# Attention value products in pairs of quads, a zero-fed opening for TensorE, and re-placed loads and steps

## Chip, core and metric

The kernel runs on one NeuronCore of one Trainium2 chip. The metric is the device time of one execution in microseconds (us), as the median of several runs. The engines are TensorE (PE, matmuls; its weight loads are shown as PEld), VectorE (DVE), ScalarE (ACT), GpSimd (POOL) and SyncE (SP), which here only issues DMAs. The text calls a busy or issue record by the line of the kernel that made it (L898 is line 898).

## The reference

32 batches of 100 queries (x, width 256) and 361 keys (ctx). Per batch:

```python
d = layernorm(x)                              # no weights
q = d @ Wq.T + bq;  k = ctx @ Wk.T + bk;  v = ctx @ Wv.T + bv     # 16 heads of 16
attn = softmax(q k^T)  (no scale);  z = attn v
x = x + (layernorm(z + d) * gamma + beta)
n = layernorm(x)
f = layernorm(n) * ln_g + ln_b
w = top 2 of 8 experts of softmax(f @ rW + rb), renormalised
x = x + n + sum_e w_e * (gelu(f @ W1_e + b1_e) @ W2_e + b2_e)
```

## The kernel before

The attention is a software pipeline over the 32 batches. Each engine runs `iteration(turn, i)` for i from -3 to 39, and each iteration has 12 **moments** s = 0 to 11. In iteration i the engines work on several batches at once: they project keys and queries of batch i+3, take row scores and row maxima of batch i+1, take transposed scores, exponentials and products with the values of batch i, and normalise batches i-1 to i-3. Where a step stands is written by hand in tables: `PE_PLACE`, `ACT_PLACE`, `DVE_PLACE`, `POOL_PLACE`, `SP_PLACE` give each step a moment (12 and more means the next iteration), `START` overrides them for batch 0 and `TAIL` for the last three. Within one moment an engine goes through its steps in the order of its `iteration` function. Places only fix the order of work on each engine; the meeting of engines is by semaphores. `SCORES_LAG, GUARD_LAG, VALUES_LAG = 3, 6, 9` place the scores, the guard and the products of a quad.

The steps that matter here, for a batch:

- **Keys** (`project_keys`, L853, PE): two fp32 products (t = 0, 1) of 361 columns each into the PSUM bank `pj[1]`. ACT writes the bf16 high part (`keys_high`, L1100) and the full value (L1104) from the bank; POOL subtracts (`k_rest`, L786), ACT makes the middle part (L1113), POOL the low part (`k_low`, L789). SP then copies the parts into `k_stack` with six DMAs of 192 KB (L653; for batch 0 in `first_stacks`, L599). Queries go the same way (L871, L1089, L1093, L793, L1109, L770) and SP copies them with six DMAs of 64 KB (L645).
- **Values** (`project_values`, L884, PE). DVE adds the bias into a tile `v_raw` (`values_biased`, L1342 and L1347) and then cleans it into `v_aug` (`values_cleaned`, L1354). `v_aug` holds each head as 16 values, a one and zeros, 32 columns in all.
- **Row scores and maxima**: 16 matmuls into two banks (`score_rows`, L898), each followed by a maximum on DVE (`row_max`, L1360). The maxima are split in three bf16 parts (`m_rows`, 48 columns) and transposed on PE (`max_transposed`, L908), copied by ACT (L1240), and stored by SP into the query stack (L635).
- **Transposed scores** (`scores`, L917): 12 groups g of four matmuls; ACT takes the exponential of each into `p_t` (`exponentials`, L1183). Three groups make a **quad** of heads. DVE guards a finished quad (`guard`, L1365).
- **Products with the values** (`values`, L929): one quad at a time, at g = 0, 3, 6, 9 with a lag of 9 moments. Twelve fp32 matmuls (24 instructions) whose weights are 32 columns wide, four of them side by side in the array. `p_t` has two slots, so the exponentials of a quad wait for the products two quads earlier.
- **z and what follows**: ACT copies z (L1254), PE transposes it (L937), DVE normalises (L1371 to L1382), SP stores it to DRAM (`zout`, L638: 1,600 pieces of 64 bytes) and loads it back (`zin`, L632), POOL adds (`u`, L798), and two layer norms follow on DVE, POOL and ACT. SP writes the result twice (`zf`, L657 and L660).

SP issues everything in one order. In an iteration this order is: zin, q, k (all moment 2), ctx (3, the load of the keys' input, L628), zout (4), zf (7), max (10). POOL's order is q_low, rstd2, k_rest, u, k_low, rstd, xb, y, q_rest, m_rest, m_low.

x comes in six loads. The first two are issued at the start. `X_LOAD_AT` gives the others to ACT (L1208); load 2 (batches 12 to 21, 1,000 KB) is issued at (i, s) = (-2, 10). The first layer norm's sums are made on DVE, one batch a time (`x_sums`, L1300), where `X_SUM_AT` says; the first of load 2 at (-1, 6). When all batches of a load are summed, eight small steps make the variance (`x_variance_step`, L1310 to L1324).

After the attention a second phase gathers tokens by expert and runs the experts over 57 tiles of 128 tokens (L976 to L999, gather L706, scatter L721). The change does not touch its work, only where some of its buffers lie.

## Time and profile before

| | |
|---|---|
| Median of 3 runs | 846.84 us (845.5 to 849.79) |
| The profiled execution, its own time | 850.93 us |
| Its span in the profile | 848.7 us |
| Mean granted clock of TensorE | 0.943 |
| PE busy | 755.9 us (89%) |
| DVE busy | 631.7 us (74%) |
| ACT busy | 563.4 us (66%) |
| POOL busy | 535.6 us (63%) |

The attention pipeline fills about the first 560 us of the span, its even stretch runs from about 188 to 515 us, and the experts' tiles take the rest. A record says how long an instruction took and, in brackets, how long its engine sat idle before it and what ended that. Matmuls overlap, so their records are longer than their distance; the chain that ended last gives the distance. Records of SPq and ACTq are the issuing of a DMA, not its transfer.

### The profile page before, as it was taken

To read this page: it belongs to the slowest core of one execution; us is meant where nothing else is said; L and a number is where in the kernel's file an instruction comes from. 1 tells how busy PE (TensorE), PEld (TensorE's weight loads), DVE (VectorE), ACT (ScalarE), POOL (GpSimd) and SP (SyncE) were. 2 spreads that over 40 slices of the span, in tenths; PEclk is the share of its full clock that TensorE was granted. 3 is DMA by queue.
4 is the path that set the end of the run, shared out by engine and by line. 5 is a ranking of instruction groups with operands and counts; after the bars stand their busy time and mean duration, and the time that the engine had idled before them with its cause. 6 is when DMAs were issued, how large, how long until landed. Compare 5 with 4: busy or idle time off the path is not lost.

```text
span 848.7 us, 26242 instructions
## 1 busy us (share of the span) xinstructions
PE 755.9 (89%) x8056; PEld 586.7 (69%) x8057; DVE 631.7 (74%) x1779; ACT 563.4 (66%) x1469; POOL 535.6 (63%) x609
## 2 busy tenths in 40 slices
PE   3689999999999999999999997565979888999994
PEld 2456667767777777777777675344968787999994
DVE  7488998889899998998998898875446673454441
ACT  3346777888888887888888885533655544666662
POOL 3323667677677676876777775317456555777773
PEclk9989999999999999999999999855989998999998
DMA  6756575768768677677687676621334333443441
GB/s 186 170 122 144 125 159 123 161 148 179 161 150 189 140 172 165 152 170 169 147 183 160 160 169 147 195 59 43 57 55 63 51 46 56 75 63 57 67 62 21
DMA packets 154000, 104.43 MB, mean 123 GB/s; under 512 B 68364, under 2 KB 149560, under 8 KB 153816
## 3 DMA queue, kind: packets, MB, share of 16 engines
q1 hardware_dynamic: 133462, 77.42, 41.8%
q0 software_dynamic: 10944, 14.10, 10.3%
q10 hardware_dynamic: 9538, 12.23, 5.1%
q8 instruction: 28, 0.46, 0.2%
q14 instruction: 28, 0.23, 0.1%
HBM read 36.65 MB, written 17.33 MB: 64 GB/s over the span
## 4 chain that ended last, share of the span: by engine, by line
PE 62%; DMA 11%; DVE 8%; issue 6%; POOL 6%; SPq 4%; ACT 2%; DVEq 1%; ACTq 0%; POOLq 0%
PE s_row L988 9%; PE pj L884 8%; PE pj L853 8%; PE s_row L898 7%; PE s_t L917 7%; PE zt L929 7%; PE pj L999 4%; PE zt L999 4%; PE pj L871 3%; SPq L653 2%; DMA stack_x<-in_x 2%; DMA out_x<-index_space,idx_s 2%; DMA zscr<-zn 2%; DVE negmax L1360 2%; DMA stack_x<-k_part 2%
## 5 line engine op out<-in xcount | busy, mean ns | idle before, releaser
L1360 DVE TENSOR_REDUCE negmax<-s_row 100x1 f32<-100x361 f32 x512 | 251.5, 524 | 24.8 <-PE s_row L898 18.9
L1183 ACT ACTIVATE p_t<-s_t 128x400 f32<-128x400 f32 x384 | 187.9, 499 | 85.8 <-PE s_t L917 77.6
L898 PE MATMUL s_row<-stack_x,q_stack 125*128 125x361 bf16 x512 | 133.2, 322 | 18.7 <-DVE negmax L1360 12.8
L721 POOL DMA_INDIRECT out_x<-index_space,idx_s x57 | 92.2, 1617 | 76.3 <-ACT index_space L1168 34.6
L917 PE MATMUL s_t<-q_stack,stack_x 128*128 128x100 bf16 x1536 | 129.4, 211 | 10.9 <-ACT p_t L1183 8.7
L917 PEld LDWEIGHTS s_t<-q_stack,stack_x 128*128 128x128 bf16 x1536 | 93.5, 99 | 57.3 <-issue 30.9
L988 PE MATMUL s_row<-w_qkv,v_aug 128*128 128x128 f32 x912 | 117.8, 285 | 1.2 <-DVE v_aug L1455 1.2
L988 PEld LDWEIGHTS s_row<-w_qkv,v_aug 128*128 128x128 f32 x912 | 113.0, 202 | 1.8 <-DVE v_aug L1455 1.7
L1365 DVE TENSOR_SCALAR p_t<-p_t 128x1200 f32<-128x1200 f32 x128 | 100.0, 781 | 12.8 <-ACT p_t L1183 12.7
L884 PE MATMUL pj<-w_qkv,ct 128*128 128x256 f32 x384 | 106.0, 399 | 0.0
L853 PE MATMUL pj<-ct,w_qkv 128*128 128x361 f32 x256 | 96.1, 500 | 10.3 <-DMA bk_s<-in_bk 9.2
L929 PE MATMUL zt<-p_t,v_aug 128*32 128x100 f32 (+1 forms) x3072 | 96.7, 261 | 1.0 <-DVE p_t L1365 1.0
L929 PEld LDWEIGHTS zt<-p_t,v_aug 128*32 128x32 f32 (+1 forms) x3072 | 67.3, 113 | 34.9 <-issue 33.3
L1162 ACT ACTIVATE w_qkv<-s_row,b_k 128x128 f32<-128x128 f32 x228 | 64.8, 367 | 27.0 <-PE s_row L988 24.5
L898 PEld LDWEIGHTS s_row<-stack_x,q_stack 125*128 125x128 bf16 x512 | 46.8, 101 | 50.5 <-DVE negmax L1360 34.8
L706 POOL DMA_INDIRECT q_part<-zf_d,idx_g x57 | 68.2, 1196 | 17.8 <-issue 15.7
L884 PEld LDWEIGHTS pj<-w_qkv,ct 128*128 128x128 f32 x384 | 66.5, 193 | 6.4 <-issue 1.1
L853 PEld LDWEIGHTS pj<-ct,w_qkv 128*128 128x128 f32 x256 | 46.0, 198 | 27.5 <-issue 11.0
L1154 ACT ACTIVATE w_qkv<-pj,lnb_c,lng_c 128x128 f32<-128x128 f32 x57 | 26.1, 457 | 51.1 <-PE pj L976 44.2
L1455 DVE TENSOR_SCALAR v_aug<-w_s 128x1024 f32 x57 | 40.2, 706 | 23.7 <-issue 22.6
L798 POOL TENSOR_TENSOR u<-z_in,td 100x256 f32<-100x256 f32 x32 | 45.7, 1427 | 18.5 <-DMA z_in<-zscr 17.8
L767 POOL TENSOR_TENSOR m_rest<-negmax,m_rows 100x16 f32<-100x16 f32 x32 | 36.4, 1139 | 32.4 <-ACT m_rows L1248 32.4
(232 smaller groups left out, 1423.8 us busy)
## 6 DMA issues: line engine op xcount, KB each, us to landing
stack_x<-k_part SPq DMA_DIRECT2D x192, 192.0 KB, 3.6
q_stack<-q_part SPq DMA_DIRECT2D x192, 64.0 KB, 2.0
ct<-in_ctx_t SPq DMA_DIRECT2D x32, 361.0 KB, 4.3
stack_x<-in_w ACTq DMA_DIRECT2D x8, 512.0 KB, 6.7
w_s<-in_w ACTq DMA_DIRECT2D x14, 256.0 KB, 2.9
zscr<-zn SPq DMA_DIRECT2D x32, 100.0 KB
z_in<-zscr SPq DMA_DIRECT2D x32, 100.0 KB
zf_d<-zf_s SPq DMA_DIRECT2D x32, 100.0 KB
```

The source lines that it names most:

```text
L706: pool.indirect_dma_start(zg[:, k.ring, :], None, zf_rows[0:n], bass.IndirectOffsetOnAxis(idx_g[:, k.ring:k.ring + 1], 0), bounds_check=n ...
L721: pool.indirect_dma_start(out_rows[0:n], bass.IndirectOffsetOnAxis(idx_s[:, k.slot:k.slot + 1], 0), ys[:, k.slot, :], None, bounds_check=n ...
L853: last = nc.tensor.matmul(pj[1][:, 0:KEYS], wk_s[:, c, t * 128:t * 128 + 128], ct[:, a.slot, c, 0:KEYS], start=(c == 0), stop=(c == 1))
L884: last = nc.tensor.matmul(bank[:, kt % 2 * D:kt % 2 * D + D], ct[:, b.slot, c, kt * 128:kt * 128 + 128], wv_s[:, c, :], start=(c == 0), st ...
L898: nc.tensor.matmul(s_row[h % 2][:, 0:KEYS], q_stack[0:MROW, b.slot, h, :], k_stack[0:MROW, b.slot, h, 0:KEYS], start=True, stop=True).then ...
L917: last = nc.tensor.matmul(s_t[g % 2][:, j * Q:j * Q + Q], k_stack[:, b.slot, h, kt * 128:kt * 128 + 128], q_stack[:, b.slot, h, 0:Q], star ...
L929: last = nc.tensor.matmul(zt[32 * j:32 * j + 32, quad * Q:quad * Q + Q], v_aug[0:n, b.slot, kt * H + 4 * quad + j, :], p_t[0:n, quad % 2, ...
L988: last = nc.tensor.matmul(p_h[k.slot][:, j * 128:j * 128 + 128], w1_k[k.slot][:, c * HF + j * 128:c * HF + j * 128 + 128], zgt[:, k.slot, ...
L999: last = nc.tensor.matmul(p_y[k.slot][:, 0:D], hidt[:, k.slot, c * 128:c * 128 + 128], w2_s[:, bass.ds(e, 1), c, :].rearrange("p e f -> p ...
L1183: nc.scalar.activation(p_t[:, quad % 2, kt, :], s_t[g % 2][:, 0:4 * Q], ACT.Exp).then_inc(exp_done, 1)
L1360: v.tensor_reduce(negmax[:, b.slot, h:h + 1], s_row[h % 2][0:Q, 0:KEYS], AXIS.X, ALU.max, negate=True).then_inc(max_done, 1)
L1365: v.tensor_scalar(p_t[:, quad % 2], p_t[:, quad % 2], 0.0, None, ALU.max).then_inc(p_ready, 1)
```

## The change

1. `values` runs two quads in one go, at g = 3 (quads 0 and 1) and g = 9 (2 and 3), and waits for the guard of the second. `p_t` gets a third slot, addressed by `ring(b, quad)`.
2. `v_raw` is gone: the bias is added straight into `v_aug`, which is then cleaned in place. Buffers of the second phase move into `k_rest` and `p_t`.
3. `m_rows` is 128 columns wide (80 of them zeros), and so is the transposition of the maxima.
4. At the start PE runs eight products of zeros (400 columns, fp32), one more after the first keys, three after the first queries. The first keys' second half goes into the bank `zt` and doesn't wait for the first half to be read; ACT reads both high parts first. PE waits only for its own weights there, not for the bias.
5. x loads 2 to 5 are issued later (load 2 at (-1, 8) in place of (-2, 10)), and their sums made five an iteration from (0, 1) on; the variance of load 2 at i = 2 in place of 1; three small loads (`later_loads`) at i = 0 in place of -1.
6. The place tables change. On SP the order becomes zin, q (moment 0), zf (1), k (5), ctx (6), zout (9), max (11). POOL's and DVE's orders stay. On ACT drow, k0, k1 and zft go ahead, the maxima's copy and q_mid go behind the next exponential. On PE dt, zft and router go ahead.

```diff
-X_LOAD_AT = {(-2, 10): 2, (0, 0): 3, (0, 6): 4, (1, 0): 5}
-X_SUM_AT = {(-1, 6 + n): 12 + n for n in range(6)}
-X_SUM_AT.update({(0, 1 + n): 18 + n for n in range(4)})
-X_SUM_AT.update({(1 + (n >= 3) + (n >= 7), (1, 3, 9, 1, 3, 9, 10, 1, 3, 9)[n]): 22 + n for n in range(10)})
+X_LOAD_AT = {(-1, 8): 2, (0, 2): 3, (0, 8): 4, (1, 2): 5}
+X_SUM_AT = {(n // 5, (1, 4, 7, 9, 10)[n % 5]): 12 + n for n in range(20)}
...
+def ring(b, quad):
+    return (b.slot + quad) % 3
...
-        p_t = sb(es, "p_t", [128, 2, KT, 4 * Q])
+        p_t = sb(es, "p_t", [128, 3, KT, 4 * Q])
-            m_rows = sb(att, "m_rows", [Q, 3 * H], BF16)
+            m_rows = sb(att, "m_rows", [Q, 128], BF16)
...
+            def keys_bank(a, t):
+                return zt if a.known and a.index == 0 and t == 1 else pj[1]
...
-                    if isinstance(turn, int) and i == -1:
+                    if isinstance(turn, int) and i == 0:
                         later_loads()
...
+                def run_idle(n):
+                    for _ in range(n):
+                        nc.tensor.matmul(tr[:, 0:G * Q], zt_s[:, 0:128], zt_s[:], start=True, stop=True)
...
-                    nc.tensor.matmul(tr[0:3 * H, 0:Q], m_rows[:], ident_bf[:], start=True, stop=True).then_inc(mt_done, 1)
+                    nc.tensor.matmul(tr[:, 0:Q], m_rows[:], ident_bf[:], start=True, stop=True).then_inc(mt_done, 1)
...
-                    pe.wait_ge(p_ready, G * b.index + quad + 1)
+                    if quad % 2 == 0:
+                        pe.wait_ge(p_ready, G * b.index + quad + 2)
...
                 pe.wait_ge(memsets, 4)
+                pe.wait_ge(zeros_ready, 1)
+                run_idle(8)
...
-                        if n.valid() and g % KT == 0:
+                        if n.valid() and g in (KT, 3 * KT):
+                            values(n, g // KT - 1)
                             values(n, g // KT)
...
-                        after(act, pv_done, G * b.index + quad - 1)
-                    nc.scalar.activation(p_t[:, quad % 2, kt, :], s_t[g % 2][:, 0:4 * Q], ACT.Exp).then_inc(exp_done, 1)
+                        after(act, pv_done, G * b.index + quad - 2)
+                    nc.scalar.activation(p_t[:, ring(b, quad), kt, :], s_t[g % 2][:, 0:4 * Q], ACT.Exp).then_inc(exp_done, 1)
...
-                    after(dve, v_ready, b.index)
+                    after(dve, pv_done, G * (b.index - 2))
...
-                    v.scalar_tensor_tensor(v_aug[:, b.slot, :, 0:DH], v_raw[:], 0.0, v_raw[:], ALU.max, ALU.min).then_inc(v_ready, 1)
+                    biased = v_aug[:, b.slot, :, 0:DH]
+                    v.scalar_tensor_tensor(biased, biased, 0.0, biased, ALU.max, ALU.min).then_inc(v_ready, 1)
...
-                        if isinstance(turn, int) and i in (1, 4) and 4 <= s < 12:
-                            x_variance_step({1: 2, 4: 3}[i], s - 4)
+                        if isinstance(turn, int) and i in (2, 4) and 4 <= s < 12:
+                            x_variance_step({2: 2, 4: 3}[i], s - 4)
...
-PE_PLACE = {"v0": 1, "v1": 2, "v2": -1, "k0": 5, "k1": 10, "dt": 3, "q": 6, "z": 7, "zft": 3, "router": 6, "max": 12}
-ACT_PLACE = {"drow": 2, "k0": 6, "k1": 11, "dt": 4, "q": 8, "q_mid": 11, "k_mid": 15, "zt": 5, "zft": 4, "td": 5, "u": 6, "y": 14, "max": 11, "m_high": 9, "m_mid": 10}
-DVE_PLACE = {"stats": 4, "var": 5, "stats2": 10, "var2": 12, "v2": 0, "v01": 1, "logits": 6, "z": 7, "v_aug": 9}
-POOL_PLACE = {"u": 1, "k_low": 15, "rstd": 3, "y": 6, "q_low": 12, "rstd2": 12, "t": 7, "k_rest": 13, "q_rest": 8, "m_rest": 10, "m_low": 11, "xb": 4}
-SP_PLACE = {"zf": 7, "ctx": 3, "q": 14, "k": 14, "zout": 4, "max": 10, "zin": 14}
+PE_PLACE = {"v0": 1, "v1": 2, "v2": -1, "k0": 5, "k1": 10, "dt": 2, "q": 6, "z": 7, "zft": 2, "router": 4, "max": 12}
+ACT_PLACE = {"drow": 1, "k0": 5, "k1": 10, "dt": 4, "q": 8, "q_mid": 12, "k_mid": 15, "zt": 5, "zft": 2, "td": 5, "u": 6, "y": 14, "max": 12, "m_high": 9, "m_mid": 10}
+DVE_PLACE = {"stats": 4, "var": 5, "stats2": 11, "var2": 12, "v2": 0, "v01": 1, "logits": 6, "z": 7, "v_aug": 10}
+POOL_PLACE = {"u": 4, "k_low": 18, "rstd": 6, "y": 7, "q_low": 13, "rstd2": 13, "t": -1, "k_rest": 15, "q_rest": 8, "m_rest": 10, "m_low": 11, "xb": 7}
+SP_PLACE = {"zf": 1, "ctx": 6, "q": 12, "k": 17, "zout": 9, "max": 11, "zin": 12}
```

`START` changes to match: k0 and k1 on PE at moment 0, dt 1, q 2; on ACT q_mid at 4; on POOL k_rest 1, q_rest 2, k_low 3, q_low 4.

## Rows read from the trace of the kernel before

**Rows 1.** Busy time by stretch: start, engine busy time and count, clock, DMA share, GB/s.

```profile
36.00:40.00 4.00, 0.89 (x9) 0.72 (x7) 0.00 (x0) 1.04 (x4) 0.56 (x1) 0.89 1.14 216
40.00:44.00 4.00, 0.00 (x0) 0.00 (x0) 0.53 (x2) 0.00 (x0) 0.00 (x0) 0.50 0.95 189
...
188.00:436.00 248.00, 247.33 (x3212) 178.16 (x3212) 225.48 (x576) 208.26 (x528) 184.74 (x241) 1.00 0.74 163
```

**Rows 2.** The chain that ended last, in order of time, one steady iteration: start, duration.

```profile
302.80 0.65 PE zt L929 x24
303.45 0.28 PE s_t L917 x4
...
307.54 0.15 PE tr L908
307.70 0.28 PE s_t L917 x4
...
309.22 0.18 PE s_t L917 x4
```

**Rows 3.** Timeline of a steady iteration, weight loads of one quad.

```profile
302.72 0.50 PEld L929 LDWEIGHTS zt<-p_t,v_aug 128*32 128x32 f32 x24 [0.16 <-issue]
```

**Rows 4.** Timeline of a steady iteration: the DMA issues of SP.

```profile
298.98 3.81 SPq L653 DMA_DIRECT2D stack_x<-k_part  x6
...
304.54 2.56 SPq L657 DMA_DIRECT2D zf_d<-zf_s  x1
...
309.09 0.30 SPq L632 DMA_DIRECT2D z_in<-zscr  x1
309.53 3.81 SPq L645 DMA_DIRECT2D q_stack<-q_part  x6
...
314.84 3.81 SPq L653 DMA_DIRECT2D stack_x<-k_part  x6
```

**Rows 5.** Who waited for whom on SP, 188 to 468 us: total, times, longest.

```profile
SPq L653 <- POOL k_part L789: 19.7, 18, 1.4
...
SPq L632 <- DMA zscr<-zn: 5.4, 15, 0.5
```

**Rows 6.** Line L657: durations of its 32 issues, ns min/median/max.

```profile
L657 SPq DMA_DIRECT2D zf_d<-zf_s x32: 288/2596/3751, 113.0 to 623.4; - x32
```

**Rows 7.** Timeline of the start: keys, queries, first row scores.

```profile
1.42 3.91 POOL L678 MEMSET v_aug<- 128x2304 f32 x2
...
9.21 2.74 PE L853 MATMUL pj<-ct,w_qkv 128*128 128x361 f32 x4 [9.21 <-DMA bk_s<-in_bk]
...
26.31 1.46 PE L853 MATMUL pj<-ct,w_qkv 128*128 128x361 f32 x4
...
28.47 0.47 PE L898 MATMUL s_row<-stack_x,q_stack 125*128 125x361 bf16 x2
```

**Rows 8.** Timeline around the second load of x by ACT.

```profile
26.23 0.33 ACTq L1208 DMA_DIRECT2D stack_x<-in_x  x1
...
34.12 3.93 SPq L653 DMA_DIRECT2D stack_x<-k_part  x6
...
34.96 0.56 ACT L1104 ACTIVATE k_rest<-pj,bk_s 128x361 f32<-128x361 f32 x1
...
43.47 0.43 DVE L1300 BATCH_NORM_STATS2 stats<-stack_x 100x6 f32<-100x256 f32 x1 [7.84 <-DMA stack_x<-in_x]
...
44.38 0.92 PE L898 MATMUL s_row<-stack_x,q_stack 125*128 125x361 bf16 x2 [7.50 <-DVE negmax L1360]
...
49.91 0.47 PE L898 MATMUL s_row<-stack_x,q_stack 125*128 125x361 bf16 x2
...
51.49 0.42 DVE L1300 BATCH_NORM_STATS2 stats<-stack_x 100x6 f32<-100x256 f32 x1
```

**Rows 9.** Timeline: the next iteration's first row scores; one step of a variance.

```profile
66.97 0.47 PE L898 MATMUL s_row<-stack_x,q_stack 125*128 125x361 bf16 x2 [1.82 <-issue]
...
123.66 0.17 DVE L1312 TENSOR_SCALAR mean<-ln 100x10 f32<-100x10 f32 x1
```

More of the change, by code:

```diff
@@ L848, in project_keys @@
                         if a.known and a.index == 0:
-                            pe.wait_ge(k_const, 32)
+                            pe.wait_ge(wk_loaded, 16)
                         pe.wait_ge(ctx_loaded[a.slot], 16 * a.turn + 16)
-                    wait_bank_free(pj_high, f"k{t}", a)
+                    if not (a.known and a.index == 0):
+                        wait_bank_free(pj_high, f"k{t}", a)
                     for c in range(2):
-                        last = nc.tensor.matmul(pj[1][:, 0:KEYS], wk_s[:, c, t * 128:t * 128 + 128],
+                        last = nc.tensor.matmul(keys_bank(a, t)[:, 0:KEYS], wk_s[:, c, t * 128:t * 128 + 128],
                                                 ct[:, a.slot, c, 0:KEYS], start=(c == 0), stop=(c == 1))
@@ L1231, in iteration @@
                                 keys_high(a, t)
+                                if not (a.known and a.index == 0):
+                                    keys_full(a, t)
+                                elif t == 1:
+                                    keys_full(a, 0)
+                                    keys_full(a, 1)
                         for d in due(turn, i, s, -1, "ACT", "td"):
```

63 lines of the change are left out of this document (36 added, 27 removed).

## Prediction

> **What bounds the kernel now.** I read the busy time by stretch first. In the even stretch, 188 to 436 us, PE is busy 247.33 of 248.00 us at a granted clock of 1.00, DVE 225.48, ACT 208.26 [rows 1]. Sixteen iterations fit in, 15.5 us each (the issue of the key copies at 298.98 and the next at 314.84 are 15.86 apart [rows 4]; over 248 us it is 15.5). So matmuls seem to fill the iteration, and what leaves PE should leave the time. The chain that ended last agrees: in this stretch it runs on PE piece after piece [rows 2].
>
> The second view is SP's own queue [rows 4, 5], and it says that PE is not alone. SP issues the key copies at 298.98, stores z behind them, and can load it back (309.09) only when the store has landed: it waited for that 15 times in 18 iterations, 5.4 us in all. Queries follow at 309.53, key copies again at 314.84, where SP waits for POOL's low parts 19.7 us in 18 iterations, 1.1 each. This is a loop. From the key copies to the load of z it takes 309.09 - 298.98 = 10.1 us, and from there to the next key copies 5.75 us here, 5.4 in the mean (15.5 - 10.1). Its slack is SP's wait for POOL alone.
>
> A rule stands against the first view. The Trainium skill (Trainium Kernel Development and Optimization, Performance Expectations) says that matmul busy time is a bad measure of the distance to the limit, because matmuls are pipelined, and that the share of weight loads is a good one; here that is 178.16 of 248.00, 72% [rows 1]. By the rule PE need not be the limit and its saving may be worth nothing; by the chain of rows 2 it is worth all of it. My sum lies near the rule, but on SP's rows.
>
> The third view is the start. DVE waits 7.84 us for the second big load of x, issued at 26.23, and holds PE for 7.50 us; the clock falls to 0.50, and the next row scores run at 0.92 us where 0.47 is usual [rows 1, 8].
>
> **Products in pairs.** A quad takes 0.65 us on the chain and the scores behind it 0.28 where they take 0.18 elsewhere [rows 2]. The weights of its 24 instructions load in 0.50 us [rows 3]. If a second quad follows at that rate without a new switch of the array's tiling, a pair costs 0.50 + 0.76 in place of 1.52: 0.26 saved, twice an iteration, 0.52. No gain would be the lower end, since only the rows of single quads exist. The wide maxima: 0.15 and 0.28 behind [rows 2] become at best a fourth of 0.18 and 0.18, so 0.2 saved; the lower end is nothing. Together 0.7 us of PE an iteration, 15.5 to 14.8. The longer wait of the pair for the second guard costs nothing, since its products stand where they stood; the first quad's exponentials have the third slot to go to. Over the 25 iterations from i = 5 to 29 that is 17.5 us if PE alone decided.
>
> **The values' bias without v_raw.** Same operations, same elements, DVE order kept: I take nothing, with at most the difference of a strided write between 0 and 0.3 us an iteration (DVE has 22.5 us free in 16 iterations [rows 1], 1.4 each). What hides it is that slack.
>
> **The new order on SP.** Ahead of the key copies now stand z's load, the queries and, new, both writes of the result. From z's load: 0.44 to the queries, 3.81 for them [rows 4], the writes, the key copies. A write that isn't held up takes 0.29 (the shortest of L657), but the median is 2.6 [rows 6], because it now follows z's 1,600 pieces. Behind the queries I take 0.3 each and 0.4 for the gaps: 0.44 + 3.81 + 1.0 = 5.3, then 10.1: the loop takes 15.4 without any wait for POOL. That is 0.13 less than now: with 25 iterations 3 us saved. Ends: if the store of z also becomes shorter and PE decides, 17.5; if a write is held 2.6 us as today, 10.1 + 4.25 + 2.6 + 0.7 = 17.6 an iteration, 53 us lost. I take 0.3, as the two issues of 64 KB ahead of it are issued at an even 0.63 each [rows 4] and nothing of 1,600 pieces is in front. The maxima's DMA is now next behind z's store; it comes with a later moment, and I take it as not held.
>
> **PE's and ACT's moves** (dt, zft, router, k0, k1, the maxima's copy). The router's wait for ACT's copy could cost PE 0.2 us an iteration; PE's 0.6 us of new slack covers it. With no slack it would cost 5 us.
>
> **The opening.** The first keys run at 2.74 us for four instructions where 1.46 is usual [rows 7], so TensorE was at its lower level (1.2 GHz). The zeros start when POOL's last memset is done, at 1.42 + 3.91 = 5.3 us [rows 7]; eight of them at 400 columns are 8 x 1.5 = 12 us at the slow rate (2.74 / 2 x 400 / 361), half that at the fast one, and I take 8. Then the first keys start 4 us later than at 9.21 but take 1.4 instead of 2.7, and the second half doesn't wait for ACT. They end about where they did, near 16. After that the clock is up, queries are 0.4 to 1 us earlier, and the first row scores come near 27.8 in place of 28.47. Ends: 2 us later, 2 us earlier.
>
> **The load of x.** Without DVE's wait, iteration -1 is 49.91 - 28.47 = 21.4, less 7.5 idle, less 2 for the low clock: 12, so batch 1's row scores could start at 40. Their key copies are issued at 34.12 and need 8 us: 41. The load is now issued where ACT has read batch 2's first keys, near 35 [rows 8]. From then DMA has 1,000 KB of x, up to 1,152 KB of key copies and 361 KB of ctx, at 216 GB/s [rows 1] 11.6 us, and the landing: 47.5 (between 45 and 52, the latter if it takes its 17.2 us again). DVE wants it at (0, 1), near 42. So a wait of 5.5 us stands in a new place, PE idles, and the clock falls again. DVE summed there at 51.49 [rows 8]; now at 47.5: 4 us saved. To the next iteration's row scores at 66.97 [rows 9] it loses 2 us by the low clock and gains the 1.82 of that row and some: 4.5 us earlier.
>
> **Sums and variance.** Five sums of 0.43 [rows 8] at i = 2 in place of four, and eight steps of 0.17 [rows 9] moved there: DVE has 14.1 us of work (225.48 / 16), plus 2.2 and 1.4 makes 17 against 15.5. An end of i = 2 that is 0.8 us later is my value; ends 0 and 2. The three small loads, 1.3 us of SP, are hidden by the wait for x.
>
> **The end of the attention**: the last pair waits for its second guard where one quad was done earlier: 0.5 us later. The experts' phase: nothing.
>
> **The sum.** -4.5 (start) + 0.8 - 3.1 + 0.5 = -6.3, and I take -6, as the last terms are rough. The profiled execution (850.93, span 848.7) lies 4.1 above the median of 846.84; the changes are taken off the median: 841 us. A measurement of this kernel can tell some 0.5%, 4.2 us, from no change.
>
> **Rivals.**
> 1. *PE decides.* z's store lands sooner, or the key copies leave more room, and the whole 17.5 us come, with the start: 846.8 - 22 = 825. For it: PE is busy 247 of 248 us, and the chain is on PE alone. Against: the 10.1 us from key copies to z's load, which the wait for z ends in 15 of 18 iterations [rows 5]. Chance 0.2.
> 2. *SP's queue decides (slower).* The result's writes ahead of the key copies cost more than 1.3 us together instead of 1.0. From that point on each tenth costs 2.5 us over 25 iterations. With one write held half as long as today, 1.3 us, an iteration takes 10.1 + 4.25 + 1.3 + 0.7 = 16.35, 0.85 more: +21 - 6 + 3 = 865; held 0.5 us more, 15.9: 854. Chance 0.15, mostly at the lower value.
> 3. *The start gives nothing.* The load takes its 17 us again and lands at 52; then only steady savings remain: 845. Chance 0.2.
>
> The Trainium skill (DMA: Bandwidth & Descriptors, Issuing engines are not separate DMA queues) says that DMAs issued from any engine run on the same 16 engines and interleave. By it, a load of x on ACT's queue can't pass the key copies that SP issues at the same time, and rival 3 would be the likelier; the share of 1.14 at 36 to 40 us [rows 1] agrees that they met.
>
> **Numbers.** Forecast 0.45, rivals 0.2, 0.15, 0.2. Faster by over 0.5% (below 842.6): two thirds of the forecast, all of rival 1 and a little of rival 3, 0.52. Slower: rival 2 and the unlucky part of rival 3, 0.18. The rest, 0.30, within 0.5%. The range, 826 to 854, leaves out half of rival 1 and the dear half of rival 2; the forecast's own range is 836 to 847.
>
> **What would show it.** Steady iterations at 15.4; SP no longer waiting for POOL at the key copies, but for z at its load; PE with gaps of 0.5 us an iteration; L657 near 0.3 us; pairs of 48 instructions 1.16 long. A wait of DVE for x near 42 us, of 4 to 7 us, and a low clock after it. It is wrong if the iteration falls to 14.8 (the loop isn't one), if L657 keeps its 2.6 us, or if the pair costs what two quads cost.

## The result and the profile after

The kernel after takes 859.57 us (median of 5 runs, 858.17 to 861.46) where the kernel before takes 846.06 (5 runs): ratio 1.0144, 95% interval 1.0123 to 1.0166. The forecast was 841, faster, with a range up to 854. It was wrong in direction and outside its range. The profiled execution of after took 861.46, span 859.7, beside 848.7 before: 11.0 us to find.

| us from the start of the span | before | after |
|---|---|---|
| maxima's transpose of batch 0 | 50.31 | 47.40 |
| of batch 2 | 83.02 | 83.77 |
| of batch 8 | 183.14 | 183.74 |
| of batch 27 | 478.27 | 479.76 |
| of batch 30 | 525.51 | 527.38 |
| first product of the experts' second layer | 597.44 | 607.70 |
| last such product | 835.56 | 846.55 |

All of it is read from one profiled execution of each kernel. The opening gains 2.9 us and has lost them by batch 2; from there to batch 30 another 1.1 are lost where 3.1 less 0.8 were forecast as a gain; between batch 30's maxima and the experts 8.4 us are lost. The last 0.7 lie between the experts' first and last product, a stretch in which the runs of this document differ by 1.7 us (237.7 to 239.4) for no cause that I know. From here on "the iteration" is the distance from batch 9's to batch 27's transpose of the maxima in the timeline, over 18: 15.53 us before, 15.59 after.

**The steady part.** Busy time by stretch of after, as [rows 1]: start, busy time and count of each engine, clock, DMA share, GB/s.

```profile
40.00:44.00 4.00, 0.00 (x0) 0.00 (x0) 0.00 (x0) 0.00 (x0) 0.00 (x0) 0.83 0.70 154
...
188.00:436.00 248.00, 240.69 (x3206) 183.15 (x3206) 223.30 (x575) 207.31 (x526) 181.23 (x240) 1.00 0.71 162
```

PE is busy 240.69 us where it was 247.33. It did get less work, and the time did not follow. The chain of after says where the next bound is:

```profile
297.12 0.49 PE tr L966 x4
...
300.76 1.03 POOL rstd L806
...
305.76 1.31 POOL m_rest L772
...
309.31 0.56 POOL q_part L775
...
311.69 0.59 ACT stack_x L1155
312.27 0.33 ACT zft L1252
...
312.74 0.31 PE tr L966 x2
```

Where [rows 2] stay on PE, this is a loop of one iteration from the router's product (L966) over row scores, DVE, POOL's long queue and ACT's copy (L1252) back to the router: 312.74 - 297.12 = 15.6 us. I called it loop L.

SP's issues in after, as [rows 4], and its waits, as [rows 5]:

```profile
300.44 3.82 SPq L658 DMA_DIRECT2D stack_x<-k_part  x6
...
310.47 0.30 SPq L637 DMA_DIRECT2D z_in<-zscr  x1
...
314.92 0.35 SPq L662 DMA_DIRECT2D zf_d<-zf_s  x1
...
315.92 0.59 SPq L658 DMA_DIRECT2D stack_x<-k_part  x1
```

```profile
SPq L640 <- ACT m_part L1269: 59.3, 18, 3.5
SPq L637 <- DMA zscr<-zn: 9.1, 18, 0.8
```

The write of the result (L662) takes 0.35 and is no longer held; key copies to z's load are 10.03 us, from there to the next key copies 5.45. SP waits for the maxima's copy 3.3 us in each iteration.

**The opening.** PE's timeline: the zeros, the first keys, the first row scores of batches 0, 1 and 2 (iterations -1, 0 and 1); in brackets the idle time before.

```profile
5.39 7.16 PE L854 MATMUL tr<-zt_s 128*128 128x400 f32 x16 [5.39 <-POOL v_aug L683]
12.38 1.38 PE L864 MATMUL pj<-ct,w_qkv 128*128 128x361 f32 x4
...
25.96 0.48 PE L909 MATMUL s_row<-stack_x,q_stack 125*128 125x361 bf16 x2
...
46.84 0.76 PE L909 MATMUL s_row<-stack_x,q_stack 125*128 125x361 bf16 x2 [9.01 <-issue]
...
66.46 0.75 PE L909 MATMUL s_row<-stack_x,q_stack 125*128 125x361 bf16 x2 [2.66 <-issue]
```

DVE's wait for x [rows 8] is gone. PE now stands 9.01 us in its place; the profile names no releaser, but the last of the key copies that these scores read landed at 46.8, just before 46.84. The row scores then take 0.76 where 0.48 is usual: the granted clock reads 0.50 from 44 to 48 us. The DMA view (issues, KB each, median us from issue to landing): before from 28 to 48 us, after in the same stretch, after in the whole run:

```profile
stack_x<-k_part SPq DMA_DIRECT2D x6, 192.0 KB, 6.8
```

```profile
stack_x<-k_part SPq DMA_DIRECT2D x6, 192.0 KB, 9.2
```

```profile
stack_x<-k_part SPq DMA_DIRECT2D x192, 192.0 KB, 3.6
```

Beside the load of 1,000 KB, key copies need 9.2 us where 3.6 are usual. In the kernel before, where the load had 8 us of lead, they already needed 6.8.

**The end of the attention.** ACT's queue at the start of iteration 30, after:

```profile
525.87 0.41 ACTq L1158 DMA_DIRECT2D stack_x<-in_w  x1
526.31 3.27 ACTq L1158 DMA_DIRECT2D stack_x<-in_w  x4
530.08 0.23 ACT L1269 ACTIVATE m_part<-tr 48x100 bf16<-48x100 f32 x1
```

The same place before:

```profile
525.77 0.25 ACT L1240 ACTIVATE m_part<-tr 48x100 bf16<-48x100 f32 x1 [0.80 <-PE tr L908]
525.78 3.97 ACTq L1134 DMA_DIRECT2D stack_x<-in_w  x5
```

The copy of the maxima (moment 11, now 12, which is moment 0 of the next iteration) has fallen behind the experts' first weight loads, which are issued there. It runs 4.3 us later (1.9 of them because the transpose itself is later), and its DMA goes out behind five loads of 512 KB of weights: on the chain it lands 6.4 us after its issue. Who waited for it from 524 to 562 us, first after, then before:

```profile
PEld s_t L929 <- DMA q_stack<-m_part: 4.9, 1, 4.9
```

```profile
PEld s_t L917 <- DMA q_stack<-m_part: 0.7, 1, 0.7
```

So 4.2 us of the 8.4 are lost here. Most of the rest is one iteration on: the kernel, late by then, stores z at 547.47, beside the next weight loads (issued from 547.20 on), and the store takes 7.3 us on the chain where before had 3.6 (at 542.47, ahead of its loads). The maxima's DMA of iteration 31 stands behind z's load on SP and goes out at 555.12.

### The profile page after: what moved, and what is told of

The parts are those of the page before. It is cut to its first block, busy times and chain, and to the rows that moved or that the text cites. A ratio compares the mean times of both kernels' runs of the same rounds, so it can differ in the third digit from the quotient of the medians.

```text
span 859.7 us, 26250 instructions
## 1 busy us (share of the span) xinstructions
PE 748.0 (87%) x8080; PEld 597.9 (70%) x8081; DVE 630.8 (73%) x1781; ACT 563.7 (66%) x1469; POOL 528.5 (61%) x609
## 4 chain that ended last, share of the span: by engine, by line
PE 34%; POOL 19%; issue 18%; DVE 14%; DMA 6%; ACT 5%; DVEq 1%; POOLq 1%; ACTq 1%
PE s_row L1001 7%; PE pj L864 5%; DVE negmax L1391 5%; DMA out_x<-p_t,idx_s 4%; POOL m_rest L772 3%; PE pj L1012 3%; PE s_row L909 3%; PE zt L1012 3%; PE pj L895 3%; POOL rstd L806 2%; POOL rstd L784 2%; PE zt L942 2%; PE s_t L929 2%; POOL y L778 2%; PE tr L966 2%
## 5 line engine op out<-in xcount | busy, mean ns | idle before, releaser
L726 POOL DMA_INDIRECT out_x<-p_t,idx_s x57 | 93.2, 1635 | 77.4 <-ACT p_t L1192 33.1
L929 PE MATMUL s_t<-q_stack,stack_x 128*128 128x100 bf16 x1536 | 124.1, 211 | 11.4 <-ACT p_t L1207 6.5
L929 PEld LDWEIGHTS s_t<-q_stack,stack_x 128*128 128x128 bf16 x1536 | 96.3, 100 | 48.0 <-issue 20.2
L1396 DVE TENSOR_SCALAR p_t<-p_t 128x1200 f32<-128x1200 f32 x128 | 99.6, 778 | 14.2 <-ACT p_t L1207 14.0
L895 PE MATMUL pj<-w_qkv,ct 128*128 128x256 f32 x384 | 107.5, 404 | 0.0
L864 PE MATMUL pj<-ct,w_qkv 128*128 128x361 f32 x252 | 88.9, 475 | 0.0
L942 PE MATMUL zt<-p_t,v_aug 128*32 128x100 f32 (+1 forms) x3072 | 83.5, 259 | 1.8 <-DVE p_t L1396 1.6
L909 PEld LDWEIGHTS s_row<-stack_x,q_stack 125*128 125x128 bf16 x512 | 44.2, 102 | 52.1 <-DVE negmax L1391 31.7
L1186 ACT ACTIVATE w_qkv<-s_row,b_k 128x128 f32<-128x128 f32 x228 | 64.6, 365 | 17.3 <-PE s_row L1001 16.1
L895 PEld LDWEIGHTS pj<-w_qkv,ct 128*128 128x128 f32 x384 | 67.3, 195 | 6.2 <-issue 0.3
L775 POOL TENSOR_TENSOR q_part<-q_rest,q_part 128x200 bf16<-128x200 f32 x32 | 18.1, 565 | 62.5 <-ACT q_part L1133 62.5
L803 POOL TENSOR_TENSOR u<-z_in,td 100x256 f32<-100x256 f32 x32 | 39.7, 1239 | 26.8 <-DMA z_in<-zscr 26.3
L1012 PE MATMUL pj<-stack_x,w_qkv 128*128 x232 | 56.0, 385 | 0.0
L1192 ACT ACTIVATE p_t<-p_t,gate 128x256 f32<-128x256 f32 x57 | 28.9, 507 | 41.1 <-DVE p_t L1499 39.6
```

Source lines behind the costliest of these rows:

```text
L726: pool.indirect_dma_start(out_rows[0:n], bass.IndirectOffsetOnAxis(idx_s[:, k.slot:k.slot + 1], 0), ys[:, k.slot, :], None, bounds_check=n ...
L864: last = nc.tensor.matmul(keys_bank(a, t)[:, 0:KEYS], wk_s[:, c, t * 128:t * 128 + 128], ct[:, a.slot, c, 0:KEYS], start=(c == 0), stop=(c ...
L895: last = nc.tensor.matmul(bank[:, kt % 2 * D:kt % 2 * D + D], ct[:, b.slot, c, kt * 128:kt * 128 + 128], wv_s[:, c, :], start=(c == 0), st ...
L909: nc.tensor.matmul(s_row[h % 2][:, 0:KEYS], q_stack[0:MROW, b.slot, h, :], k_stack[0:MROW, b.slot, h, 0:KEYS], start=True, stop=True).then ...
L929: last = nc.tensor.matmul(s_t[g % 2][:, j * Q:j * Q + Q], k_stack[:, b.slot, h, kt * 128:kt * 128 + 128], q_stack[:, b.slot, h, 0:Q], star ...
L942: last = nc.tensor.matmul(zt[32 * j:32 * j + 32, quad * Q:quad * Q + Q], v_aug[0:n, b.slot, kt * H + 4 * quad + j, :], p_t[0:n, ring(b, qu ...
```

## Experiments

Each is compared with the kernel before on the same chip; ratios, not medians, compare runs of different groups.

| run | edit | us | ratio to before, 95% | iteration |
|---|---|---|---|---|
| after | | 859.57 | 1.0144 (1.0123 to 1.0166) | 15.59 |
| e1_act_max | ACT's copy at 11 | 860.58 | 1.0139 (1.0095 to 1.0183) | 16.03 |
| e2_loads_later | weights one moment later | 852.99 | 1.0042 (1.0010 to 1.0073) | 15.59 |
| e4_xload_early | load of x earlier | 858.95 | 1.0111 (1.0067 to 1.0155) | 15.63 |
| e5_old_places | all places of before | 855.20 | 1.0076 (1.0051 to 1.0102) | 15.68 |
| e6_zft_late | e2, zft and router late | 853.15 | 1.0047 (1.0024 to 1.0070) | 15.62 |
| e7_zft_late_ctx | e6, ctx late | 850.81 | 1.0008 (0.9981 to 1.0035) | 15.59 |
| e8_single_quads | e2, quads single | 865.54 | 1.0207 (1.0183 to 1.0232) | 16.13 |
| e9_x_in_fives | e6, x in pieces | 859.97 | 1.0130 (1.0099 to 1.0161) | 15.62 |
| e10_short_guard | e7, one guard short | 846.81 | 0.9968 (0.9951 to 0.9985) | 15.59 |
| e11_v01_late | e7, bias later | 853.84 | 1.0066 (1.0040 to 1.0092) | 15.80 |
| e12_x_as_before | e7, x as before | 848.63 | 1.0001 (0.9981 to 1.0021) | 15.58 |
| e13_split_bias | e12, bias in halves | 852.95 | 1.0037 (1.0014 to 1.0059) | 15.74 |
| e14_rows_spread | e12, last row later | 857.45 | 1.0092 (1.0057 to 1.0127) | 15.89 |
| e15_both | e13 and e14 | 867.00 | 1.0212 (1.0165 to 1.0258) | 16.08 |
| e16_old_places_quads | e5, quads single | 845.72 | 0.9955 (0.9937 to 0.9973) | 15.32 |
| e17_quads_x_before | e16, x as before | 844.41 | 0.9956 (0.9935 to 0.9976) | 15.32 |
| e18_pair_first | e17, quads 1, 2 paired | 839.60 | 0.9888 (0.9871 to 0.9905) | 15.20 |
| e19_pair_second | e17, quads 3, 4 paired | 860.09 | 1.0129 (1.0106 to 1.0152) | 15.82 |

**The end and the opening: e1, e2, e4, e9, e12.**

```diff
-ACT_PLACE = {..., "max": 12, ...}
+ACT_PLACE = {..., "max": 11, ...}
```

> The kernel after with one place changed: ACT copies the transposed maxima at moment 11 again, not 12. Theory T (the tail): the kernel after loses some 9 us between 525 and 600 us because the copy now stands behind ACT's five loads of expert weights in iteration 30, so that the maxima's DMA to the query stack lands 6.4 us after its issue at 530.3 (before: issued 526.0, ahead of them). By it this kernel takes 850 to 855 us, and that DMA is issued ahead of the loads. Rival (the pairs delay the tail): the last quads wait for their second guard, the time stays at 858 to 860. Rival (SP's order): 858 to 860 too.

From batch 30's maxima to the first product of the second layer it took 71.98 us, beside 80.3 in after and 71.9 before: the end came out as theory T has it. But the iteration grew to 16.03, so the whole stayed. With the rest of after's places, ACT waits for PE at this copy (L1269 for tr, 14.2 us in 248), and loop L behind it gets longer. The move from 11 to 12 paid for itself in the steady part and cost 8.4 us at the end.

```diff
-                    if isinstance(turn, int) and i in WEIGHT_LOADS:
-                        load_weights(i)
                     for s in range(NG):
                         at = moment(turn, i, s)
+                        if isinstance(turn, int) and i in WEIGHT_LOADS and s == 1:
+                            load_weights(i)
```

> The kernel after with ACT's loads of expert weights in iterations 27, 30 and 31 issued at moment 1 in place of ahead of moment 0, so behind the maxima's copy; nothing else. Theory T: the maxima's DMAs meet no weights in iteration 30, and the tail gets shorter as in the first experiment or more, 849 to 855 us. Rivals (pairs, SP's order): 858 to 860.

This keeps the move and lets the copy go first: 72.3 us for the end, the iteration unchanged, and the ratio falls from 1.0144 to 1.0042. The loss at the end is this one order on ACT's queue: with it the copy at iteration 30 isn't held, and the store of z at iteration 31 (544.85) takes 3.3 us again.

```diff
-X_LOAD_AT = {(-1, 8): 2, (0, 2): 3, (0, 8): 4, (1, 2): 5}
+X_LOAD_AT = {(-2, 10): 2, (0, 2): 3, (0, 8): 4, (1, 2): 5}
```

> The kernel after with load 2 of x issued at (-2, 10) as before; its sums stay where the kernel after has them, from (0, 1). Theory S (the start): in the kernel after the load, issued at 31.8 us, runs beside the key copies issued at 31.4, whose landing holds PE for 9.0 us until 46.8. With the load out early neither DVE nor the key copies wait: the row scores of iteration 0 start near 41, and 4 to 6 us are saved, 853.5 to 855.5. Rival: the key copies land late for another reason, 859.

Nothing was gained that the intervals can tell (1.0111 beside after's 1.0144). The load, issued at 24.96, met the query copies issued at 25.24: the last of them landed 7.95 us after its issue (2.0 is usual), DVE waited 8.36 us for row scores of batch 0, and batch 2's maxima came at 83.0.

```diff
-X_LOADS = [..., slice(12, 22), slice(22, 25), slice(25, 29), slice(29, B)]
-X_LOAD_AT = {(-1, 8): 2, (0, 2): 3, (0, 8): 4, (1, 2): 5}
+X_LOADS = [..., slice(12, 17), slice(17, 22), slice(22, 27), slice(27, B)]
+X_LOAD_AT = {(-1, 8): 2, (0, 8): 3, (1, 2): 4, (1, 8): 5}
```

> e6_zft_late with the later loads of x in four pieces of five rows of the batch (500 KB each) at (-1,8), (0,8), (1,2), (1,8) in place of ten rows, then 3, 4 and 3. Theory S2 (the key copies of batch 1, issued beside the load of 1,000 KB, land late because they share the DMA engines with it: 4.7 us usual, 15 here): half the load lets them land near 42 to 43 in place of 46.6, row scores of batch 0 near 43 to 44, and 3 us less in all against e6. Rival S3 (what is gained there is given back by iteration 0 or 1, as the 3 us that the kernel after gained at this place were gone at the row scores of batch 2): row scores of batch 2 where they are in e6 within 0.7 us, and the time the same.

Batch 0 gained (its maxima at 44.82), but the later pieces of 500 KB stood beside later copies: DVE waited 5.87 us for row scores near 89, and batch 2's maxima came at 89.4, 6 us after e6's 83.1. Theory S2 has the mechanism and not the sum: each big load delays whatever stack copies run beside it, and smaller pieces hit more of them.

```diff
-X_LOAD_AT = {(-1, 8): 2, (0, 2): 3, (0, 8): 4, (1, 2): 5}
+X_LOAD_AT = {(-2, 10): 2, (0, 0): 3, (0, 6): 4, (1, 0): 5}
```

(with the sums, the variance and SP's later loads as before)

> e7_zft_late_ctx with the later loads of x, their sums, the variance of the second part and SP's later loads at the moments of the kernel before. Theory S3 (the place of the load of x moves the idle time and doesn't remove it: it delays the stack copies issued beside it, by some 8 to 10 us in the kernel after, or is waited for by VectorE, 7.8 us in the kernel before): row scores of batch 0 at 48 to 50 in place of 47, those of batch 2 within 1 us of those of e7, and the time the same within 1.5 us. Theory S (my prediction: the later load is worth 4 us): 3 to 4 us slower than e7.

The ratio is 1.0001 beside e7's 1.0008, and e17 below repeats it (0.9956 beside e16's 0.9955). The place of the load is worth nothing, within about 0.3% in each of the two comparisons, where theory S, mine in the prediction, has 3 to 4 us, over 0.4%. It is refuted.

**Loops around the iteration: e6, e7, e10.**

```diff
-PE_PLACE = {..., "zft": 2, "router": 4, ...}   ACT_PLACE = {..., "zft": 2, ...}
+PE_PLACE = {..., "zft": 3, "router": 6, ...}   ACT_PLACE = {..., "zft": 4, ...}
```

> The kernel after, with the weights' loads one step later (so that its base is e2_loads_later: steady iteration 15.59, time 852.99), and PE's zft and router and ACT's copy of zft back at moments 3, 6 and 4. Theory L (a loop decides the steady iteration: maxima's split on POOL 1.3 and its rest, q_low, rstd2 and gain on POOL, y on ACT in moment 2, transpose of zft on PE and its copy on ACT in the same moment, then PE's next keys and row scores): with a moment between them the waits of PE for ACT at zft and at the router (18 us over 248 in the kernel after) go to under 5, the iteration falls to 15.2 to 15.4, 4 to 8 us less in all, time near 847. Theory A (SP and DMA loop of key copies, z's store, z's load): PE's waits for ACT go too, but the iteration stays at 15.5 or more and the time at 851 to 854, with the idle time of PE in other places.

PE's waits for ACT at zft and the router, 18 us together in after, fell to 2.0. The iteration stayed: 15.62. The chain left POOL and went back to PE and DVE. Loop L was on the chain and was not the reason.

```diff
-SP_PLACE = {..., "ctx": 6, ...}
+SP_PLACE = {..., "ctx": 10, ...}
```

> e6_zft_late and, on SP, the context's load at moment 10 in place of 6, so that it no longer lies between the key copies and the store of z (361 KB, about 2 us of DMA time at 200 GB/s). Theory A: from key copies to the load of z 8 to 8.5 us in place of 10.0, and the iteration falls by 0.3 to 1 us below that of e6, 8 us less or more in all. Theory L: key copies to z's load shorter too, but the iteration stays within 0.1 of that of e6, since SP then waits for its other partners (POOL's low parts or ACT's copy of the maxima) that much longer.

The iteration is 15.59, within 0.03 of e6. From key copies to z's load it came out at 9.75 us, not 8.5, since z's load stands behind the maxima's DMA, and that waits for ACT. So the stretch was shortened by only 0.3, a weak test. But SP has 35.0 us of waits for ACT in 18 iterations, and a loop with that slack decides nothing. Of the 0.4% in time 1.9 us lie at the end in the two traces (from batch 30's maxima to the first product of the second layer 71.5 us, e6 73.4) and 0.9 ahead of it; I have no cause for them.

```diff
-                    v.tensor_scalar(p_t[:, ring(b, quad)], ...)
+                    guarded = p_t[:, ring(b, quad)] if quad != 3 else p_t[:, ring(b, quad), 0, 0:Q]
+                    v.tensor_scalar(guarded, ...)
```

> e7_zft_late_ctx with the guard of the fourth quad (VectorE, 128x1200, 0.78 us) done on 128x100 only, about 0.2 us: VectorE's work falls by 0.6 us an iteration. It leaves the clamp of that quad's exponentials out, apart from its first hundred columns. Theory D (what pairs took off TensorE is held back by VectorE: it has 14.0 us of work and some 1.5 of waits in its order, and in e7 the row scores wait for its row maxima twice in each iteration, since there are two banks for them; the steady chain of e7 shows two pieces of DVE negmax per iteration where that of the kernel before shows none): the iteration falls from 15.59 by 0.2 to 0.5 us, 5 to 13 us in all. Rival (TensorE alone: busy 243 of 248 us): it has at most 0.3 us idle, and the iteration falls by less than 0.1. A fall of 0.3 exactly would be both: TensorE's full rate, 15.28.

The iteration stayed at 15.59. But the test is weaker than planned: the short guard took 0.53 us, not 0.2, so VectorE lost 0.25 us of work an iteration in place of 0.6 (220.23 busy in 248 us, e7 224.08). That none of it arrived, and that its wait for row scores grew instead (14.2 us, e7 9.1), speaks against VectorE's total as the bound. The 0.4% in time have no cause that I know. In the traces they lie ahead of batch 8 (its maxima at 180.39, e7 183.38), but e12 is as early there (179.97) and no faster than e7 by its ratio.

**Places against pairs: e8, e5, e16.** The edit of e8 (on e2) and e16 (on e5) is the same (and each quad waits for its own guard):

```diff
-                        if n.valid() and g in (KT, 3 * KT):
-                            values(n, g // KT - 1)
+                        if n.valid() and g % KT == 0:
                             values(n, g // KT)
```

> e2_loads_later with the products with the values one quad at a time again (each at its own moment, waiting for its own guard), third place for the exponentials, early places and wide maxima kept. Pairs save 2 x 0.26 us of TensorE's time an iteration by the profile (a quad 0.65 on the chain, 1.5 for two; a pair 1.17 to 1.24). If that saving reaches the iteration's length, e8 takes 0.3 to 0.5 us an iteration more than e2 (15.9 to 16.1, 861 to 865 us). If the loop over POOL and ACT decides (theory L), single quads cost at most 0.15 an iteration and e8 is at 853 to 857, with less idle time on PE and the same period.

> The kernel after with all five place tables of before (START, the x loads, the pairs, the wide maxima and the zeros stay). Theory A (the loop of SP and DMA, key copies to z's load to key copies, 10.1 plus 5.3 to 5.5 us): the steady iteration stays near 15.4, since z's store and load still close the loop; with the tail of before back the time is 843 to 850. Rival P (PE decides, the new places hold it): the iteration falls to 14.9 and the time to 832 to 838.

> e5_old_places (all five tables of places of the kernel before, everything else of the change) with single quads again. What is left of the change is then the opening, the wide maxima, the values without v_raw and the third slot. If these are neutral in the steady part, the iteration is 15.45 to 15.55, that of the kernel before (15.53), and pairs at the old places cost 0.15 us an iteration (e5: 15.68) where they save 0.54 at the new ones (e8). If it is 15.8 or more, one of these parts costs time by itself and the new places and the pairs only buy it back; then pairs save 0.2 or more at the old places too.

The four corners, iteration in us:

| | single quads | pairs |
|---|---|---|
| places of before | 15.32 (e16) | 15.68 (e5) |
| places of after | 16.13 (e8) | 15.59 (e2) |

With the new places pairs save 0.54, with the old ones they cost 0.36. e5 came out as neither of its theories had it (15.4 or 14.9); e8 is just above the upper end of its own (16.1). That 0.54 is nearly the 0.52 of the prediction may be luck: PE is not full in e2 or in e8 (240.69 and 241.18 busy of 248), and e2's chain runs over POOL and ACT. And the new places cost 0.81 where quads are single; no run takes them one by one.

e16, 15.32, is the rest of the change on its own, against 15.53 before: a gain of 0.21, where its expectation had 15.45 to 15.55. From there the change goes to the opposite corner, e2, and pays 0.27 for it. The chain of e16 shows one source of the gain, the wide maxima:

```profile
306.90 0.05 PE tr L920
306.95 0.18 PE s_t L929 x4
```

beside 0.15 and 0.28 [rows 2]: 0.20 us an iteration, as much as the whole gain, though no run has the width alone. PE is full in e16:

```profile
188.00:436.00 248.00, 247.32 (x3247) 180.52 (x3248) 226.99 (x583) 212.92 (x534) 186.93 (x243) 1.00 0.75 164
```

**Why pairs cost: theory P.** The chain of e5 leaves PE behind the values' last projection (L895), for DVE's bias and two row maxima, and comes back at a row score (the first line is a pair of quads):

```profile
308.46 1.17 PE zt L942 x48
...
312.01 0.94 PE pj L895 x4
...
313.04 0.07 DVE v_aug L1378
...
313.65 0.97 DVE negmax L1391 x2
...
314.67 0.33 PE s_row L909
```

In e16 the same stretch runs on PE, and what stands in it is a quad (L941):

```profile
308.55 0.93 PE pj L895 x4
309.48 0.31 PE s_row L909 x2
309.79 0.65 PE zt L941 x24
310.44 0.28 PE s_t L929 x4
...
311.26 0.31 PE s_row L909 x2
```

There are two banks for row scores, so the second of moment 4 needs the maximum of the second of moment 2. From the projection's end to it DVE needs 1.7 us (bias 0.69, two maxima of 0.49, the gaps; 312.95 to 314.67 in e5). PE's work in between is 1.9 us with the quad of moment 3 (from 309.48 to the second score, near 311.4) and 1.2 without. The pair took the quad away to moment 6, and PE stands about half a microsecond. The score that had to be waited for then takes 0.33 on the chain where one of two in a row takes 0.16.

Attempts to make room in other ways failed:

```diff
-DVE_PLACE = {..., "v01": 1, ...}
+DVE_PLACE = {..., "v01": 2, ...}
```

> e7_zft_late_ctx with the bias of the first two thirds of the values (VectorE, 0.69 us) one moment later, behind the next two row maxima in place of ahead of them. Theory D: VectorE's wait of 0.28 us for the projection is filled, and the row scores at that place no longer wait for maxima behind the bias: the iteration falls by 0.1 to 0.3 us, 2 to 7 us in all. Rival: the wait moves to another place of the ring (the projection of the keys needs the bank that the bias reads), and the iteration stays within 0.05.

15.80: no fall, and worse than the rival too.

```diff
-                        for b in due(turn, i, s, 1, "DVE", "v01"):
-                            values_biased(b, False)
+                        for b in due(turn, i, s, 1, "DVE", "v0"):
+                            values_biased_half(b, 0)
+                        for b in due(turn, i, s, 1, "DVE", "v01"):
+                            values_biased_half(b, 1)
```

> e12_x_as_before with the bias of the first two thirds of the values (VectorE, 0.69 us) in two halves of some 0.41: the first where the whole stood, the second one moment later, behind the next two row maxima. Theory P (two places in the iteration decide, at which the row scores wait for the maxima of those before them: one behind this bias, with 0.3 to 0.4 us lost, one behind the queries' projection): the maxima come 0.28 us sooner, and the iteration falls from 15.58 by 0.15 to 0.3, although VectorE has 0.13 us more work. Rival (TensorE's work and the order as a whole): the iteration stays within 0.05, or grows by the 0.13.

```diff
-ROW_COUNTS = (2, 2, 2, 0, 2, 2, 2, 2, 2, 0, 0, 0)
+ROW_COUNTS = (2, 2, 2, 0, 2, 2, 2, 2, 1, 1, 0, 0)
```

> e12_x_as_before with the sixteenth row score and row maximum at moment 9 in place of 8 (and one step of the routing one moment later for it). Theory P: the wait of the row scores behind the queries and z's transposes (0.4 to 0.5 us for the maximum of the moment before) is halved, and the iteration falls by 0.1 to 0.4 us. Rival: the maxima's split on ACT and POOL starts later by as much and hands the time on to the next batch's loop, and the iteration stays at 15.55 or more.

> e13_split_bias and e14_rows_spread in one. Theory P: both gains add, down to TensorE's own work of 15.15 to 15.3 us an iteration, time 838 to 842. Rival: within 0.1 of 15.58, 847 to 850.

15.74, 15.89 and 16.08 where theory P had falls. In e13 POOL waits 18.4 us for DVE's variance where e12 has 7.7, and in about a third of the iterations the chain goes over POOL as in loop L. In e14 POOL waits 28.5 us for ACT's m_rows, which e12 had at 17.3. These runs speak against P's numbers. That later steps of DVE made other loops longer is what these waits suggest and not shown; the quad itself they don't touch. The last group does:

```diff
-                        if n.valid() and g % KT == 0:
+                        if n.valid() and g == 3:
+                            values(n, 0)
+                        if n.valid() and g % KT == 0 and g != 0:
                             values(n, g // KT)
```

(e18: quads 1 and 2 together at moment 0; e19 has 9, 2 and 6 in place of 3, 0 and 0: quads 3 and 4 together at moment 6)

> e16_old_places_quads with the later loads of x, their sums and the variance at the moments of the kernel before. Theory S3 (the load of x at either place costs about the same): within 1.5 us of e16's 845.7. But e12 came out 2 us below e7 with the same edit; if that holds, 842 to 844, and the moved load of x was a loss in the change, not the gain of 4 us that I forecast.

> e17_quads_x_before with only the first two quads of a batch as a pair (at moment 0; the third and fourth stay single at moments 3 and 6). Theory P (a quad between the row scores of moments 2 and 4 covers VectorE's bias and maxima): no wait of the row scores at moment 4, TensorE's saving of 0.26 us arrives at least in part, the iteration is 15.05 to 15.3, and the time 836 to 842. Rival (any pair crowds the row scores, since VectorE's maxima set their pace everywhere): 15.4 to 15.5.

> e17_quads_x_before with only the third and fourth quad of a batch as a pair (at moment 6; the first and second single at moments 9 and 0), so that no quad stands at moment 3. Theory P: nearly the whole loss of the two pairs is here, the iteration is 15.45 to 15.7, the time 846 to 851. Rival: half of it, the same as e18.

The first pair alone saves 0.12 us an iteration, the second alone costs 0.50. Together -0.12 + 0.50 = 0.38; e5 against e16 has 0.36. Theory P is right about the place. PE's timeline from the row scores of moment 2 to the router's product, e17 and then e19:

```profile
304.45 0.47 PE L911 MATMUL s_row<-stack_x,q_stack 125*128 125x361 bf16 x2
304.85 0.72 PE L943 MATMUL zt<-p_t,v_aug 128*32 128x100 f32 x24
...
306.24 0.47 PE L911 MATMUL s_row<-stack_x,q_stack 125*128 125x361 bf16 x2
306.55 1.38 PE L866 MATMUL pj<-ct,w_qkv 128*128 128x361 f32 x4
...
309.18 0.48 PE L967 MATMUL tr<-rw_s,zft 128*100 128x8 f32 x4
```

```profile
311.92 0.47 PE L911 MATMUL s_row<-stack_x,q_stack 125*128 125x361 bf16 x2
...
313.38 0.77 PE L911 MATMUL s_row<-stack_x,q_stack 125*128 125x361 bf16 x2
313.99 1.39 PE L866 MATMUL pj<-ct,w_qkv 128*128 128x361 f32 x4
...
317.15 0.48 PE L967 MATMUL tr<-rw_s,zft 128*100 128x8 f32 x4
```

The two scores of moment 4 take 0.77 instead of 0.47. These lines also give the size. From the scores of moment 2 to the keys (L866) behind those of moment 4 PE takes 2.10 us in e17 and 2.07 in e19 (2.10 and 2.08 in the mean of 15 iterations), though 0.75 us of work is gone from there: the quad's 0.65, and 0.10 of the scores behind it. That work stood in a stall and was free. From the keys to the router (L967) it is 2.63 and 3.16 (2.66 and 3.19 in the mean): the second quad of the pair costs 0.53. 0.53 - 0.02 is the 0.50 that e19 lost. My expectation for it (15.45 to 15.7, 846 to 851 us) was too low, since it let the pair's saving of 0.26 arrive. In neither e5 nor e19 does the profile show PE waiting for a guard from 188 to 436 us, so the pair's wait for its second guard is not the cause.

e18 is faster than both kernels: 839.6 us, ratio 0.9888. Its 0.12 come short of the pair's 0.26. The chain of e18 shows what seems to be the next bound:

```profile
297.43 5.16 DMA zscr<-zn
...
302.61 1.99 DMA z_in<-zscr
...
304.73 1.24 POOL u L805
...
306.25 1.58 POOL k_part L796
...
307.84 0.58 SPq L660
...
312.73 5.17 DMA zscr<-zn
```

This is the loop of [rows 4, 5], closed over POOL: z stored, loaded, u, keys' low parts, key copies, z stored again 15.3 us later. From 188 to 436 us no piece of PE, DVE or ACT stands on the chain. No run makes this loop shorter, so that it holds the rest back is argued and not shown. Against e17 the time fell by 4.8 us (0.7% by the ratios), of which 0.12 x 25 = 3 are these iterations; the rest isn't assigned.

## Why the prediction was wrong

In the terms of the sum, as the profiled runs have them up to the first product of the second layer: the start was forecast at -4.5 and came out at +0.75; the steady part with the variance at 0.8 - 3.1, and came out at +1.1; the end at 0.5, and came out at 8.4. So the largest failed step is the end of the attention, the next the load of x, the third the pairs and the loop. All three were taken for a gain or for almost nothing.

- **Products in pairs.** The size was right: a pair of 48 takes 1.17 us on the chain of e5, forecast 1.16. That e8 against e2 has 0.54, forecast 0.52, may be luck, as said. The step that failed here is the sentence "The longer wait of the pair for the second guard costs nothing, since its products stand where they stood". The second quad of each pair stands there; the first was moved from moments 9 and 3 to 0 and 6. I asked what the pair waits for, and not what its first quad had been covering where it stood. At moment 3 that is DVE's bias and two maxima. Taking it from there freed nothing, and the pair's second quad costs 0.53: 0.50 us an iteration (e19).
- **Wide maxima**: 0.2 forecast, 0.2 seen on the chain, 0.21 for all that e16 keeps of the change. v_raw's removal at nothing agrees with this: DVE's bias (0.69 and 0.42) and its cleaning (0.95) take what they took.
- **SP's loop.** Key copies to z's load 10.1, measured 10.03; the write 0.3, measured 0.35; SP's waits have the form forecast (none for POOL, 0.5 us each for z). The forecast iteration of 15.4 was missed by 0.2, since SP was not what decided: it waits 3.3 us in each iteration for ACT's copy of the maxima, whose DMA the prediction took "as not held". The term of -3.1 came out as +1.1. The loop is there, though, and seems to decide in e18, on whose chain it stands alone.
- **Matmul busy time** says little here: PE is busy 97% of the stretch in after and in e8 (241.18 of 248), and their iterations differ by 0.54 us. With the rule of the Trainium skill (Trainium Kernel Development and Optimization, Performance Expectations) that it is a bad measure the traces agree. The share of weight loads does no better here: 72% before and 74% in after, whose iteration is longer.
- **PE's and ACT's moves.** I priced the router's wait at 0.2 and hidden. It was measured at 18 us over 248 with zft's and stood on the chain, but taking it away (e6) brought nothing: hidden, as said, behind the other bound. What I left out is the price of the whole set of new places with single quads, 0.81 (e8 against e16).
- **The opening**: zeros 7.16 us (forecast 8), first keys at the usual 1.38 from 12.38, first row scores at 25.96 (forecast 27.8). Right or better.
- **The load of x**: -4.5 forecast in all, +0.75 by batch 2. I let the key copies land at 41, 8 us after their issue at 34.12 (which is 42), and added the load behind them. They met, and the copies landed at 46.8. The trace of before had this already: its key copies, issued from 34.1 to 37.4 beside the load, landed 4.6 to 10.1 us later, the last at 47.5. Even there 8 us was too little for the last of them. Of rival 3 the price came true (the start gives nothing) and not the way: DVE summed x at 48.56 without a wait for it, and PE waited for the keys. The Trainium skill (DMA: Bandwidth & Descriptors, Queues, rings and completion order) says that each engine goes round-robin between the queues that have work for it; the 9.2 us of key copies beside the load fit this, though no run shows the turns.
- **Sums and variance**: 0.8 forecast; nothing is seen of it. From batch 2's maxima to batch 8's it is 99.97 us in after and 100.12 before. The prediction's own terms, 14.1 + 2.2 + 1.4, make 17.7 and not 17.
- **The end of the attention**: 0.5 us forecast, 8.4 lost in the profile, shown by e2. The prediction had only the last pair's second guard in this term. The queue that I did not look at is ACT's: moment 12 is moment 0 of the next iteration, and in iterations 30 and 31 weight loads are issued there.

The two misses of sign, the quad and the copy, have one form: an operation was moved past a boundary, and I priced the operation and not its neighbours at the place it left and the place it went to.

## What to carry to other kernels

Where two engines pass small tiles through two banks, look at the work between one tile and the next but one, not at the mean: work that seems to be in the way can be what covers the partner. Before grouping instructions, mark in the timeline what stands in each hole that they leave, and group only those that cover nobody's wait where they stand; here one pair of two was worth 0.7% and the other cost 1.7%. For every place that changes by one step, list what the loop's edge holds in its first and last passes: rare loads there cost nothing in the middle of the kernel and all of it at the end. Look where a large load lands beside copies that are waited for: here, on ACT's queue, none of the places tried was free.

## What the hardware showed that I had not expected

- A transpose of the maxima to 128 rows instead of 48 costs PE less, 0.05 in place of 0.15 on the chain, and the scores behind it 0.18 in place of 0.28: so the dear part seems to be the change of the array's form, not the rows. In a pair the second quad adds 1.17 - 0.65 = 0.52 us.
- Beside one load of 1,000 KB on ACT's queue, SP's copies of 192 KB land after 9.2 us (median of six) instead of 3.6, and one of 64 KB, in e4, after 7.95 instead of 2.0.
- The clock stayed at 1.00 over the steady stretch in each kernel whose row is shown, PE busy 240 or 247 of 248 us. In the idle 40 to 44 us of after it reads 0.83 where before had 0.50 [rows 1], although PE did nothing there in either; it had stopped at 37.8 us in after and at 36.9 before.
